# Vision tower with routed experts: expert tiles of 256 rows instead of 128, groups of 30, 25 and 10 token tiles

## The chip, the cores and the metric

One core of one Trainium2 chip. The metric is the device time of one execution in microseconds (us), the median of three runs.

## The reference, cut to what matters

Input x has 32 images of 256 channels, 64 x 64 pixels. A tokenizer turns patches of 4 x 4 pixels into 256 tokens an image by a small attention inside each patch; a class token is put ahead. Then come a tanh recurrence over the images and, last, a mixture of 8 experts on 32 x 257 = 8224 tokens of 256 channels:

```python
logits = tokens.astype(jnp.float32) @ router_w.astype(jnp.float32).T
probs = jax.nn.softmax(logits, axis=-1)
rw, re = jax.lax.top_k(probs, TOP_K)          # TOP_K = 2
rw = rw / jnp.maximum(rw.sum(-1, keepdims=True), 1e-12)
combine = jnp.zeros((N, E), tokens.dtype).at[jnp.arange(N)[:, None], re].set(rw)
out = tokens
for e in range(E):                            # E = 8
    h = jax.nn.gelu(tokens @ w1[e] + b1[e], approximate=False)
    y = h @ w2[e] + b2[e]
    out = out + combine[:, e:e + 1] * y
```

The tokens of the experts are layer-normed; their output is added to the stream before the norm.

## The kernel before

**Two blocks.** The first, the tokens stage, runs 64 units of 128 tokens through a software pipeline of 69 slots (`over_slots`), plus a 65th token tile with the 32 class tokens. In slot k tile k-4 gets its norm, its router logits, and is stored to DRAM twice: `base_dram` (the stream, with the token added) and `rows_dram` (the normed rows).

**Routing by groups.** The 65 token tiles are cut into groups of SIZES = 26, 24, 15. When a group's logits are there, `route_piece` (line 347) works on DVE in eight pieces, one a slot (`pieces_now`, in slots FIRST+SIZE+4 and on): softmax, the best two experts, ranks within an expert (`route_ranks`, PE), and from them for each token two slots in a table sorted by expert, each expert's part rounded up to whole tiles of 128 rows. `experts_of` writes the expert of each tile to `etab`. A group of n token tiles has at most (256 n + 8 x 127) // 128 expert tiles: 59, 55, 37, together 151. `xs_dram` is that table, one for each group; it is cleared with zeros by SP in pieces of three tiles, one a slot, and then `scatter` (line 301) writes each token's row to its two slots with two indirect DMAs from POOL. Group 0 is scattered in the tokens stage (two token tiles a slot in slots 38 to 50), the others at the start of the second block. `weights_high` and `weights_low` split the 64-fold weights into two float16 halves in slots 65 to 68.

**The expert stage** (the second block) has a step k for each expert tile, written out for each engine in its own order:

- SP (one queue, in order): `load_x(k + AHEAD)` into one of XT buffers; `store_y(k - 1)`; `load_base(t)` for the finals whose step is k + 4; `store_out(t)` for those whose step is k - 3.
- PE: `turn_x(k + 4)`, transposes of x in float32; `first(k + 2)`, twelve matmuls of 128 columns with high and low halves of x and w1 (lines 1404 to 1406); `second(k)`, six matmuls of 256 columns (1418 to 1420); then it reads the expert of tile k + 3 to a register (`expert`).
- ACT: `turned(k + 4)`, the float16 copy of the transposed x (1351); `gelus(k + 2)`, two gelus of 128 columns to g32 (1362).
- DVE: `y_in(k - 1)` (1459), bias added; `halves(k + 1)`, a cast of g32 to gh (1443) and the rest to gl (1445); `low(k + 4)`, the low half of x (1449); then `final(t)` (1463) for the finals of step k.
- POOL: scatters of groups 1 and 2, each with its row load, then for all token tiles `gather(t)` (1323): two indirect DMAs that fetch the two y rows of each token.

`final(t)` multiplies the two gathered rows by their gates: mid = y1 * gate + base (1467), fin = y2 * gate + mid (1472). y1, y2, hb and fin have RF = 5 buffers each. So the gather of t waits for f_done of t-5, `load_base(t)` waits for f_mid of t-5 (1287), and fin of t waits until the store of t-5 has landed (1471). The gathers of a group wait until all its y tiles are stored. `final_step` (1250) spreads the finals of groups 0 and 1 evenly over the tiles of the group behind; the 15 of the last group (`LATE`) follow after the last step.

XT, AHEAD, YS are 10, 7 and 6. PSUM: two banks for transposes (TT), three for the first layer (L1), two for y (Y).

Of the kernel before, what the change touches and what calls it, by code (L numbers as in the profile page):

```python
# [38 lines left out]
ROW = 2 * C  # L39
# [71 lines left out]
def vit_tower(nc, xc_in, xp_in, cls_tok, ln_q_w, ln_q_b, wqT, ln_kv_w, ln_kv_w_col, ln_kv_b, wk, wvT, projT, proj_b,  # L111
# [3 lines left out]
    xs_dram = [nc.dram_tensor(f"xs{g}_dram", [TILES[g] * P, C], F32, kind="Internal").ap() for g in GROUPS]  # L115
    ys_dram = [nc.dram_tensor(f"ys{g}_dram", [TILES[g] * P, C], F32, kind="Internal").ap() for g in GROUPS]
    ctx = ExitStack()
    with ctx:
# [28 lines left out]
        cnt = {n: sb(n, [P, E]) for n in "ke kr kf off off128 upto".split()}  # L147
# [153 lines left out]
        def scatter(pool, t, xrow=xrow, xrow_in=xrow_in, sent=sent, first=0):  # L301
# [5 lines left out]
            pool.wait_ge(clear[g], 16 * ((TILES[g] + 2) // 3))  # L307
# [39 lines left out]
        def route_piece(dve, g, part):  # L347
# [47 lines left out]
            if part == 5:  # L395
                dve.wait_ge(s["rk_done"], g + 1)
                step(dve.tensor_scalar(cnt["ke"][:, :], ranks_s[:, n * E:(n + 1) * E], 1.0 / P, (P - 1.0) / P - 0.49609375,
# [5 lines left out]
                step(dve.tensor_scalar(cnt["off128"][:, :], cnt["off"][:, :], float(P), None, ALU.mult))  # L403
            if part == 6:
                step(dve.tensor_tensor(S["rk"], ranks_s[:, 0:n * E].rearrange("p (t e) -> p t e", e=E),
                                       cnt["off128"][:, :].unsqueeze(1).to_broadcast([P, n, E]), ALU.add))
# [28 lines left out]
        def _(sp):  # L435
# [29 lines left out]
            pieces = [(g, q, min(q + 3, TILES[g])) for g in GROUPS for q in range(0, TILES[g], 3)]  # L465
# [746 lines left out]
        LAST = SIZES[-1]  # L1212
# [4 lines left out]
        xt = [sb(f"xt{i}", [P, C]) for i in range(XT)]  # L1217
        xT = [sb(f"xT{i}", [P, ROW], F16) for i in range(3)]
        g32 = [sb(f"g32_{i}", [P, C]) for i in range(2)]
        gh = [sb(f"gh{i}", [P, C], F16) for i in range(2)]  # L1220
        gl = [sb(f"gl{i}", [P, C], F16) for i in range(2)]
        y_s = [sb(f"y_s{i}", [P, C]) for i in range(YS)]
# [7 lines left out]
        names = "tt_ps xl_done xT_done l1_ps g_done gh_done gl_done y_ps y_done f_mid f_done".split()  # L1230
# [26 lines left out]
        LATE = range(T_ALL - LAST, T_ALL)  # L1257
# [9 lines left out]
        def _(sp):  # L1267
            def load_x(sp, k):
# [9 lines left out]
                sp.dma_start(xt[k % XT][:, :], xs_dram[g][j * P:(j + 1) * P, :]).then_inc(x_in[k % XT], 16)  # L1278

            def store_y(sp, k):  # L1280
                g, j = tile_of(k)
                sp.wait_ge(s["y_done"], k + 1)
                sp.dma_start(ys_dram[g][j * P:(j + 1) * P, :], y_s[k % YS][:, :]).then_inc(y_out[k % YS], 16)
# [62 lines left out]
        def _(act):  # L1346
            def turned(act, k):
# [3 lines left out]
                act.activation(xT[k % 3][:, 0:C], TT[k % 2][:, 0:C], ACT.Copy).then_inc(s["xT_done"], 1)  # L1351

            def gelus(act, k):
# [5 lines left out]
                if k >= 2:  # L1359
                    act.wait_ge(s["gl_done"], k - 1)  # L1360
                for m in range(CC):
                    act.activation(g32[k % 2][:, m * P:(m + 1) * P], L1[k % 3][:, m * P:(m + 1) * P], ACT.Gelu,  # L1362
                                   bias=b1_s[:, bass.ds(e, 1), m:m + 1].rearrange("p e n -> p (e n)"),
                                   scale=1.0 / WSC).then_inc(s["g_done"], 1)
# [12 lines left out]
        def _(pe):  # L1377
            mm = pe.matmul

            def turn_x(pe, k):  # L1380
# [3 lines left out]
                for q in range(CC):  # L1384
                    last = pe.transpose(TT[k % 2][:, q * P:(q + 1) * P], xt[k % XT][:, q * P:(q + 1) * P], ident[:, :])  # L1385
# [8 lines left out]
            def first(pe, k, e):  # L1394
                pe.wait_ge(s["xl_done"], k + 1)
                if k >= 3:
                    pe.wait_ge(s["g_done"], 2 * (k - 2))
                for m in range(CC):
                    o = L1[k % 3][:, m * P:(m + 1) * P]
                    for c in range(CC):  # L1400
                        wh = w1h[:, bass.ds(e, 1), c, m * P:(m + 1) * P].rearrange("p e n -> p (e n)")
                        wl = w1l[:, bass.ds(e, 1), c, m * P:(m + 1) * P].rearrange("p e n -> p (e n)")
                        xh, xl = xT[k % 3][:, c * P:(c + 1) * P], xT[k % 3][:, C + c * P:C + (c + 1) * P]
# [5 lines left out]
            def second(pe, k, e):  # L1409
# [3 lines left out]
                o = Y[k % 2][:, 0:C]  # L1413
                for m in range(CC):
                    h, l = gh[k % 2][:, m * P:(m + 1) * P], gl[k % 2][:, m * P:(m + 1) * P]
                    wh = w2h[:, bass.ds(e, 1), m, :].rearrange("p e n -> p (e n)")
                    wl = w2l[:, bass.ds(e, 1), m, :].rearrange("p e n -> p (e n)")
                    mm(o, h, wh, start=(m == 0), stop=False)  # L1418
                    mm(o, h, wl, start=False, stop=False)  # L1419
                    last = mm(o, l, wh, start=False, stop=(m == CC - 1))  # L1420
# [17 lines left out]
        def _(dve):  # L1438
            def halves(dve, k):
                dve.wait_ge(s["g_done"], 2 * k + 2)  # L1440
# [96 lines left out]
```

## Time and profile before

| | us |
|---|---|
| median of 3 runs (1655.04 to 1662.23) | 1656.12 |
| the profiled execution | 1680.15 |
| its span, first to last instruction | 1678.3 |
| PE busy in the span | 1414.3 (84%) |
| DVE busy | 1099.1 (65%) |
| ACT busy | 806.3 (48%) |
| POOL busy | 708.2 (42%) |
| mean granted TensorE clock | 0.955 |

A row of a group of instructions gives the line, engine, operation, output<-inputs, shapes and count, then busy time, the mean of one in ns, and the idle time ahead of them with what ended it. In order of time a row begins with its start and duration. PE's matmuls are pipelined: the distance between starts tells their pace, not their duration. A clock of 1.00 is 2.4 GHz, 0.50 is 1.2 GHz.

### The profile page before, as it was taken

The numbers are of one execution on the slowest core, as the hardware profiler recorded it, in microseconds if no ns is written. First come the engines' busy times: TensorE is split into PE (matmuls) and PEld (weight loads), VectorE is DVE, ScalarE is ACT, GpSimd is POOL, SyncE is SP. The second block draws the span as 40 slices with busy tenths as digits, with TensorE's granted clock in tenths as the row PEclk, the third lists the DMA queues.
The fourth block names the chain that finished last, engine by engine and source line by source line (L and its number), as shares of the span: only waits on it lengthen the run. The fifth ranks groups of instructions, "written<-read, shape, count | busy, mean of one in ns | idle before, by whom it ended". The sixth has DMA issues, their size and how long they took to land. (4 is left out here: it accounts for less than half of the span.)

```text
span 1678.3 us, 65455 instructions
## 1 busy us (share of the span) xinstructions
PE 1414.3 (84%) x25781; PEld 1083.8 (65%) x25781; DVE 1099.1 (65%) x3070; ACT 806.3 (48%) x2022; POOL 708.2 (42%) x858
## 2 busy tenths in 40 slices
PE   3799999999998989989898989989648888888870
PEld 2577777777777766777676667677536566555550
DVE  3567666766665767866676667777447556776773
ACT  1365565655554655555555556556443333333330
POOL 1233343333333433356655534334147734332536
PEclk9899999999998999999999999999869999999995
DMA  8977787877776876889999786673257646675866
GB/s 285 345 263 279 249 298 259 301 258 272 283 274 241 306 254 237 296 275 316 317 312 324 268 290 257 218 252 133 76 164 229 220 152 182 201 211 172 251 207 178
DMA packets 202089, 415.69 MB, mean 248 GB/s; under 512 B 25952, under 2 KB 126624, under 8 KB 201664
## 3 DMA queue, kind: packets, MB, share of 16 engines
q1 hardware_dynamic: 187504, 372.69, 64.7%
q0 software_dynamic: 14288, 38.82, 7.8%
q8 instruction: 214, 3.51, 0.8%
q14 instruction: 83, 0.68, 0.1%
HBM read 329.52 MB, written 81.89 MB: 245 GB/s over the span
## 5 line engine op out<-in xcount | busy, mean ns | idle before, releaser
L1039 DVE BATCH_NORM_STATS2 st<-xp 128x6 f32<-128x512 f32 x512 | 339.1, 694 | 0.5
L537 POOL TENSOR_TENSOR rs_px<-px_ve,half_neg 128x16 f32<-128x16 f32 x64 | 186.3, 2911 | 296.8 <-DVE px_ve L1044 296.8
L649 ACT ACTIVATE zT<-bank 128x512 f32<-128x512 f32 x256 | 146.2, 598 | 193.0 <-PE bank L872 192.9
L1332 POOL DMA_INDIRECT y<-ys_dram,slot x130 | 125.3, 964 | 188.4 <-DMA ys_dram<-y_s 84.4
L872 PE MATMUL bank<-ident,z_s 128*128 128x128 f32 x1024 | 163.4, 295 | 28.3 <-issue 27.5
L642 ACT ACTIVATE z_s<-bank 128x512 f32<-128x512 f32 x256 | 138.7, 597 | 61.4 <-PE bank L862 61.4
L623 ACT ACTIVATE u<-bank 128x512 f32<-128x512 f32 x256 | 132.2, 603 | 53.6 <-PE bank L812 53.6
L872 PEld LDWEIGHTS bank<-ident,z_s 128*128 128x128 f32 x1024 | 120.8, 149 | 46.9 <-issue 40.2
L832 PE MATMUL bank<-xc,u 128*32 128x64 f32 x8192 | 133.9, 220 | 18.2 <-issue 17.5
L832 PEld LDWEIGHTS bank<-xc,u 128*32 128x32 f32 x8192 | 128.0, 110 | 32.8 <-issue 21.0
L310 POOL DMA_INDIRECT xs_dram<-xrow,slot x130 | 128.4, 988 | 40.3 <-issue 37.5
L1362 ACT ACTIVATE g<-bank,b_s 128x128 f32<-128x128 f32 x302 | 94.6, 363 | 103.9 <-PE bank L1406 99.7
L862 PE MATMUL bank<-xp,pd 64*32 64x256 f32 x4096 | 140.1, 383 | 3.2 <-ACT u L623 3.2
L1404 PE MATMUL bank<-xT,xp 128*128 128x128 f16 x604 | 136.9, 227 | 1.3 <-issue 0.5
L1406 PE MATMUL bank<-xT,xp 128*128 128x128 f16 x604 | 137.1, 227 | 0.0
L1459 DVE SCALAR_TENSOR_TENSOR y_s<-bank,b_rep 128x256 f32<-128x256 f32 x151 | 64.1, 424 | 105.6 <-PE bank L1420 93.5
L1405 PE MATMUL bank<-xT,xp 128*128 128x128 f16 x604 | 133.0, 220 | 0.0
L784 PE MATMUL bank<-xp,spread 128*32 128x256 f32 x2048 | 127.7, 391 | 1.3 <-DVE cvec L1031 1.3
L522 POOL TENSOR_TENSOR q_rs<-q_ve,half_neg 128x1 f32<-128x1 f32 x64 | 35.5, 555 | 216.5 <-DVE q_ve L1056 216.2
L1351 ACT ACTIVATE xT<-bank 128x256 f16<-128x256 f32 x151 | 57.9, 383 | 140.0 <-PE bank L1385 140.0
L1385 PE MATMUL bank<-ident,xt 128*128 128x128 f32 x302 | 62.7, 290 | 69.6 <-issue 55.7
L1108 DVE TENSOR_TENSOR h_s<-bank,rc 128x256 f32<-128x256 f32 x64 | 27.2, 425 | 131.2 <-PE bank L891 131.2
(179 smaller groups left out, 3134.6 us busy)
## 6 DMA issues: line engine op xcount, KB each, us to landing
xp<-xpix SPq DMA_DIRECT2D x256, 512.0 KB
xc<-xg SPq DMA_DIRECT2D x256, 512.0 KB
xt<-xs_dram SPq DMA_DIRECT2D x151, 128.0 KB, 3.3
ys_dram<-y_s SPq DMA_DIRECT2D x151, 128.0 KB, 2.6
xs_dram<-zero SPq DMA_DIRECT2D x49, 384.0 KB, 8.2
base_dram<-h SPq DMA_DIRECT2D x65, 128.0 KB, 7.9
rows_dram<-tok SPq DMA_DIRECT2D x65, 128.0 KB, 7.6
hb<-base_dram SPq DMA_DIRECT2D x65, 128.0 KB, 3.0
```

The costliest lines, as they stand in the source:

```text
L310: pool.indirect_dma_start(xs_dram[g], bass.IndirectOffsetOnAxis(ap=slot_u[k][0:n, t:t + 1], axis=0), xrow[i][0:n, :], None).then_inc(sent[ ...
L537: pool.tensor_tensor(rs_px[:, :], px_ve[:, :], half_neg[:, :], ALU.pow).then_inc(s["px_done"], 1)
L623: act.activation(uv[:, k, :, :, :], BIG[k][:, :].rearrange("p (m a t) -> p m a t", m=CC, t=TS), ACT.Copy).then_inc(s["u_done"], 1)
L642: act.activation(z_s[:, r, 2 * half:2 * half + 2, :].rearrange("p a c -> p (a c)"), BIG[2 * r + half][:, :], ACT.Copy).then_inc(s["z_done" ...
L649: act.activation(zT[:, c, :, :].rearrange("p h (a r t) -> p r h a t", r=2, t=TS)[:, r, :, :, :], BIG[f][:, :].rearrange("p (a h t) -> p h ...
L832: last = mm(SB[32 * k:32 * k + 32, (2 * n + r) * SUB:(2 * n + r + 1) * SUB], u_s[u.two][:, c, g, :, :].rearrange("p h t -> p (h t)"), xc[u ...
L862: last = mm(BIG[2 * r + half][32 * k:32 * k + 32, n * C:(n + 1) * C], pd[64 * r:64 * r + 64, g, :, :].rearrange("p h t -> p (h t)"), xp[v. ...
L872: last = pe.transpose(BIG[f][:, n * P:(n + 1) * P], z_s[:, r, n, c * P:(c + 1) * P], ident[:, :])
L1039: dve.bn_stats(st[:, j, :], xp[u.x][:, 2 * j:2 * j + 2, :].rearrange("p i c -> p c i")).then_inc(s["st_done"], 1)
L1404: mm(o, wh, xh, start=(c == 0), stop=False)
L1405: mm(o, wh, xl, start=False, stop=False)
L1406: last = mm(o, wl, xh, start=False, stop=(c == CC - 1))
```

## The change

An expert tile has WIDE = 256 rows, two to a partition (row 2p and 2p+1 of the table in partition p), so x and y move in transfers of 256 KB, with 2 KB to a partition. The first layer's matmuls move 256 columns for each weight load, the second layer runs twice over halves of the tile. The upper half gh comes from a second gelu on ACT with a float16 output instead of DVE's cast. SIZES become 30, 25, 10, TILES 37, 32, 17 (86 together). XT, AHEAD, YS become 8, 5, 5; RF stays 5. The finals follow a new rule: one each 0.75 step, the first three steps after the last tile of their group, as many as end before the last step.

```diff
-SIZES = [26, 24, 15]
+SIZES = [30, 25, 10]
...
-TILES = [(2 * P * n + E * (P - 1)) // P for n in SIZES]
+WIDE = 2 * P
+TILES = [(2 * P * n + E * (WIDE - 1)) // WIDE for n in SIZES]
...
-            pool.wait_ge(clear[g], 16 * ((TILES[g] + 2) // 3))
+            pool.wait_ge(clear[g], 16 * ((2 * TILES[g] + 2) // 3))
...
-            pieces = [(g, q, min(q + 3, TILES[g])) for g in GROUPS for q in range(0, TILES[g], 3)]
+            pieces = [(g, q, min(q + 3, 2 * TILES[g])) for g in GROUPS for q in range(0, 2 * TILES[g], 3)]
...
-        XT, AHEAD, RF, RX2, YS = 10, 7, 5, 4, 6
+        XT, AHEAD, RF, RX2, YS = 8, 5, 5, 4, 5
...
-        final_step = {FIRST[g - 1] + i: BEFORE[g] + 5 + (TILES[g] - 5) * i // SIZES[g - 1]
-                      for g in GROUPS if g > 0 for i in range(SIZES[g - 1])}
+        ready, final_step = [0.0], {}
+        for t in range(T_ALL):
+            ready.append(max(ready[-1] + 0.75, BEFORE[group_of(t)] + TILES[group_of(t)] + 3.0))
+            if ready[-1] < N:
+                final_step[t] = int(ready[-1]) + 1
...
-        LATE = range(T_ALL - LAST, T_ALL)
+        LATE = range(len(final_step), T_ALL)
...
+                src = xs_dram[g][j * WIDE:(j + 1) * WIDE, :].rearrange("(p i) c -> p i c", i=2)
+                sp.dma_start(xt[k % XT][:, :, :], src).then_inc(x_in[k % XT], 16)
...
-                act.activation(xT[k % 3][:, 0:C], TT[k % 2][:, 0:C], ACT.Copy).then_inc(s["xT_done"], 1)
+                act.activation(xT[k % 3][:, 0, :, :], TT[k % 2][:, :].rearrange("p (c n) -> p c n", c=CC),
+                               ACT.Copy).then_inc(s["xT_done"], 1)
...
+                if k >= 3:
+                    act.wait_ge(s["y_ps"], k - 2)
                 for m in range(CC):
+                    for dst in (g32[k % 2], gh[k % 3]):
+                        act.activation(dst[:, m, :], L1[k % 3][:, m * WIDE:(m + 1) * WIDE], ACT.Gelu,
...
                 for q in range(CC):
+                    for i in range(2):
+                        last = pe.transpose(TT[k % 2][:, (2 * q + i) * P:(2 * q + i + 1) * P],
+                                            xt[k % XT][:, i, q * P:(q + 1) * P], ident[:, :])
...
+                        xh, xl = xT[k % 3][:, 0, c, :], xT[k % 3][:, 1, c, :]
                         mm(o, wh, xh, start=(c == 0), stop=False)
                         mm(o, wh, xl, start=False, stop=False)
                         last = mm(o, wl, xh, start=False, stop=(c == CC - 1))
...
+                for i in range(2):
+                    o = Y[k % 2][:, i * C:(i + 1) * C]
+                    for m in range(CC):
+                        h, l = gh[k % 3][:, m, i * P:(i + 1) * P], gl[k % 2][:, m, i * P:(i + 1) * P]
...
-                dve.tensor_copy(gh[k % 2][:, :], g32[k % 2][:, :]).then_inc(s["gh_done"], 1)
-                dve.wait_ge(s["gh_done"], k + 1)
-                dve.tensor_tensor(gl[k % 2][:, :], g32[k % 2][:, :], gh[k % 2][:, :], ALU.subtract).then_inc(s["gl_done"], 1)
+                dve.tensor_tensor(gl[k % 2][:, :, :], g32[k % 2][:, :, :], gh[k % 3][:, :, :],
+                                  ALU.subtract).then_inc(s["gl_done"], 1)
...
+                dve.scalar_tensor_tensor(y_s[k % YS][:, :, :], Y[k % 2][:, :].rearrange("p (i c) -> p i c", i=2), 1.0 / WSC,
+                                         b2_rep[:, bass.ds(e, 1), :].to_broadcast([P, 2, C]),
+                                         ALU.mult, ALU.add).then_inc(s["y_done"], 1)
```

The routing's constants follow the tile of 256 rows (1/256 in place of 1/128).

## Rows read from the trace of the kernel before

**Rows 1.** In order of time: first and last of the expert stage (start, us)

```profile
1239.53 0.69 PE L1385 MATMUL bank<-ident,xt 128*128 128x128 f32 x2 [5.08 <-DMA xt<-xs_dram]
...
1632.85 0.42 DVE L1459 SCALAR_TENSOR_TENSOR y_s<-bank,b_rep 128x256 f32<-128x256 f32 x1 [0.43 <-issue]
```

**Rows 2.** Busy time by window; columns as in its heading

```profile
core 0: us, PE busy (x) PEld busy (x) DVE busy (x) ACT busy (x) POOL busy (x), PEclk, DMA share, GB/s
...
1420.00:1520.00 100.00, 83.45 (x764) 59.35 (x763) 71.32 (x192) 38.41 (x114) 35.09 (x37) 1.00 0.70 204
1545.00:1625.00 80.00, 67.71 (x619) 47.97 (x618) 62.12 (x166) 31.35 (x93) 44.29 (x46) 1.00 0.83 247
```

**Rows 3.** PE in order of time, one tile

```profile
1376.08 0.41 PE L1385 MATMUL bank<-ident,xt 128*128 128x128 f32 x2 [0.29 <-issue]
...
1377.46 0.27 PE L1418 MATMUL bank<-xp,gh 128*128 x1
...
1378.00 0.27 PE L1420 MATMUL bank<-xp,gl 128*128 x1
1378.60 0.41 PE L1385 MATMUL bank<-ident,xt 128*128 128x128 f32 x2 [0.33 <-issue]
```

**Rows 4.** Groups of ACT and DVE by form, whole span

```profile
L649 ACT ACTIVATE zT<-bank 128x512 f32<-128x512 f32 x256 | 146.2, 598 | 193.0 <-PE bank L872 192.9
...
L1362 ACT ACTIVATE g<-bank,b_s 128x128 f32<-128x128 f32 x302 | 94.6, 363 | 103.9 <-PE bank L1406 99.7 <-DVE gl L1445 4.1
L1351 ACT ACTIVATE xT<-bank 128x256 f16<-128x256 f32 x151 | 57.9, 383 | 140.0 <-PE bank L1385 140.0
...
L1067 DVE TENSOR_TENSOR sm<-bank,fold 128x512 f32<-128x512 f32 x64 | 43.6, 682 | 11.8 <-PE bank L832 11.8
```

**Rows 5.** DVE and SP in order of time, late expert stage and tail

```profile
1601.63 0.48 DVE L1472 SCALAR_TENSOR_TENSOR fin<-y,gate,mid 128x256 f32<-128x256 f32 x1
1602.55 0.42 DVE L1459 SCALAR_TENSOR_TENSOR y_s<-bank,b_rep 128x256 f32<-128x256 f32 x1 [0.44 <-issue]
...
1634.77 1.89 SPq L1288 DMA_DIRECT2D hb<-base_dram  x4
```

**Rows 6.** DMA issues (median us to landing): 1420-1520, 1545-1625, tail, span

```profile
xt<-xs_dram SPq DMA_DIRECT2D x38, 128.0 KB, 3.5
...
tower_out<-fin SPq DMA_DIRECT2D x20, 128.0 KB, 2.9
...
tower_out<-fin SPq DMA_DIRECT2D x19, 128.0 KB, 3.4
...
tower_out<-fin SPq DMA_DIRECT2D x14, 128.0 KB, 2.2
...
xc<-w SPq DMA_DIRECT2D x16, 256.0 KB, 4.2
```

**Rows 7.** A gap of PE in the tokens stage, and the window behind it

```profile
1113.80 1.01 PE L872 MATMUL bank<-ident,z_s 128*128 128x128 f32 x4 [3.08 <-issue]
...
1113.00:1117.00 4.00, 3.20 (x21) 2.49 (x21) 0.79 (x2) 1.45 (x3) 0.00 (x0) 0.57 1.02 408
```

**Rows 8.** POOL in order of time: first and last of the 30 tail gathers

```profile
1635.67 0.94 POOL L1332 DMA_INDIRECT y<-ys_dram,slot  x1 [16.18 <-DMA ys_dram<-y_s]
...
1673.13 0.87 POOL L1332 DMA_INDIRECT y<-ys_dram,slot  x1 [0.30 <-issue]
```

**Rows 9.** DVE in order of time, drain of the tokens stage

```profile
1200.17 3.05 DVE L1163 SCALAR_TENSOR_TENSOR xp<-xc,xp 128x512 f16<-128x512 f32 x4 [0.39 <-ACT xp L696]
```

**Rows 10.** DVE in order of time: pd of two quiet slots, two with scatters

```profile
552.34 0.69 DVE L1099 TENSOR_TENSOR pd<-bank,rs_own 128x512 f32<-128x512 f32 x1 [0.32 <-PE bank L848]
...
568.96 0.69 DVE L1099 TENSOR_TENSOR pd<-bank,rs_own 128x512 f32<-128x512 f32 x1 [0.19 <-PE bank L848]
...
772.43 0.69 DVE L1099 TENSOR_TENSOR pd<-bank,rs_own 128x512 f32<-128x512 f32 x1 [0.30 <-PE bank L848]
...
790.41 0.69 DVE L1099 TENSOR_TENSOR pd<-bank,rs_own 128x512 f32<-128x512 f32 x1 [0.33 <-PE bank L848]
```

More of the change, by code:

```diff
@@ L114, in vit_tower @@
     rows_dram = nc.dram_tensor("rows_dram", [T_ALL, P, C], F32, kind="Internal").ap()
-    xs_dram = [nc.dram_tensor(f"xs{g}_dram", [TILES[g] * P, C], F32, kind="Internal").ap() for g in GROUPS]
-    ys_dram = [nc.dram_tensor(f"ys{g}_dram", [TILES[g] * P, C], F32, kind="Internal").ap() for g in GROUPS]
+    xs_dram = [nc.dram_tensor(f"xs{g}_dram", [TILES[g] * WIDE, C], F32, kind="Internal").ap() for g in GROUPS]
+    ys_dram = [nc.dram_tensor(f"ys{g}_dram", [TILES[g] * WIDE, C], F32, kind="Internal").ap() for g in GROUPS]
     ctx = ExitStack()
@@ L146, in vit_tower @@
         tiny = {n: sb(n, [P, NMAX]) for n in "lmx lsum lrec m1 i1 m2 i2 msum mcl mrec s1 s2".split()}
-        cnt = {n: sb(n, [P, E]) for n in "ke kr kf off off128 upto".split()}
+        cnt = {n: sb(n, [P, E]) for n in "ke kr kf off offw upto".split()}
         offm = sb("offm", [P, E, E])
@@ L402, in route_piece @@
                 step(dve.tensor_reduce(cnt["off"][:, :], offm[:, :, :], X, ALU.add))
[L403 removed]
+                step(dve.tensor_scalar(cnt["offw"][:, :], cnt["off"][:, :], float(WIDE), None, ALU.mult))
             if part == 6:
                 step(dve.tensor_tensor(S["rk"], ranks_s[:, 0:n * E].rearrange("p (t e) -> p t e", e=E),
[L406 removed]
+                                       cnt["offw"][:, :].unsqueeze(1).to_broadcast([P, n, E]), ALU.add))
                 for k in range(2):
@@ L1211, in vit_tower @@
         N = TILES_ALL
-        LAST = SIZES[-1]
         BEFORE = [sum(TILES[:g]) for g in GROUPS]
-        XT, AHEAD, RF, RX2, YS = 10, 7, 5, 4, 6
+        XT, AHEAD, RF, RX2, YS = 8, 5, 5, 4, 5
         xrow2 = [sb(f"xrow2_{i}", [P, C]) for i in range(RX2)]
         b2_rep = sb("b2_rep", [P, E, C])
[L1217 to L1222, printed above, removed]
+        xt = [sb(f"xt{i}", [P, 2, C]) for i in range(XT)]
+        xT = [sb(f"xT{i}", [P, 2, CC, WIDE], F16) for i in range(3)]
+        g32 = [sb(f"g32_{i}", [P, CC, WIDE]) for i in range(2)]
+        gh = [sb(f"gh{i}", [P, CC, WIDE], F16) for i in range(3)]
+        gl = [sb(f"gl{i}", [P, CC, WIDE], F16) for i in range(2)]
+        y_s = [sb(f"y_s{i}", [P, 2, C]) for i in range(YS)]
         y1 = [sb(f"y1_{i}", [P, C]) for i in range(RF)]
@@ L1282, in store_y @@
                 sp.wait_ge(s["y_done"], k + 1)
-                sp.dma_start(ys_dram[g][j * P:(j + 1) * P, :], y_s[k % YS][:, :]).then_inc(y_out[k % YS], 16)
+                dst = ys_dram[g][j * WIDE:(j + 1) * WIDE, :].rearrange("(p i) c -> p i c", i=2)
+                sp.dma_start(dst, y_s[k % YS][:, :, :]).then_inc(y_out[k % YS], 16)
             def load_base(sp, t):
@@ L1412, in second @@
                     pe.wait_ge(s["y_done"], k - 1)
[L1413 to L1420, printed above, removed]
+                for i in range(2):
+                    o = Y[k % 2][:, i * C:(i + 1) * C]
+                    for m in range(CC):
+                        h, l = gh[k % 3][:, m, i * P:(i + 1) * P], gl[k % 2][:, m, i * P:(i + 1) * P]
+                        wh = w2h[:, bass.ds(e, 1), m, :].rearrange("p e n -> p (e n)")
+                        wl = w2l[:, bass.ds(e, 1), m, :].rearrange("p e n -> p (e n)")
+                        mm(o, h, wh, start=(m == 0), stop=False)
+                        mm(o, h, wl, start=False, stop=False)
+                        last = mm(o, l, wh, start=False, stop=(m == CC - 1))
                 last.then_inc(s["y_ps"], 1)
```

24 lines of the change are left out of this document (9 added, 15 removed).

## The prediction

> **What bounds the kernel now.** I read the stages first. The last block, the expert stage, runs from the first transposes that have their data to the end of the last y_s at 1633.3 [rows 1]: 393.8 us for 151 tiles, 2.61 us each, and 45.1 us of tail follow to the end of the span at 1678.3. In the stretches by window [rows 2] PE is busy 83% at full clock while DVE has 71% and the DMA engines 0.70 (third quarter), later 78% and 0.83. Then one tile in order of time [rows 3]: from one pair of transposes to the next 2.52 us. The transposes take 0.24, the first layer with its hand-over 1.14 (12 matmuls of 128 columns), the six second-layer matmuls of 256 columns 0.108 each = 0.65, and from the end of the last one (1378.11) to the next transposes 0.49 go by, PE's register load and waits. So PE's own stream sets the tile; the other 0.09 to 2.61 is small stalls. Not in the rows of before, but in the code: SP runs one queue in which the load of x for a later tile stands behind waits for the final additions.
>
> **The change, part by part.**
>
> *PE step.* Tiles go from 151 to 37+32+17 = 86 of double size. Four transposes 0.53 (two: 0.24 to 0.27), first layer 12 x 256 columns and second 12 x 256, at the second layer's 0.108: 2.59; hand-over 0.11, overhead 0.49, stalls 0.08 as before: 3.80. 86 x 3.80 = 327, and 2 to fill. Taken alone that saves 65 us. Bounds for the pitch of the 256-column first layer: 0.095 (its pitch at 128 columns, 1.14/12) and 0.27, the duration of one 256-column matmul if none overlapped; the second layer's 0.108 is the same shape, so I take it. The Trainium skill ("TensorE: Matmul & The Clock Gate", Back-to-back issue gap) gives 81 ns at 128 columns and 131 at 512; read between, 98 at 256. The case's row says 108 for 256, so the measurement decides; by the page the steps would be 21 us shorter in all.
>
> *ACT, DVE.* ACT per step: one copy of 512 columns at 0.60 (as zT), and four gelus of 256 columns. A copy grew by 0.215 from 256 to 512 columns, so 128 more add 0.11 to the gelu's 0.36: 4 x 0.47 = 1.9. Together 2.5 of 3.8, hidden by PE; two tiles of before took 2.2, so without cover it would cost 0.3 a step. DVE: three operations of 512 elements at 0.68 (as sm), the cast gone: 2.0. A final is mid and fin, 0.5 each [rows 4, 5]. At 4 finals in 3 steps that makes 3.4 per step: hidden, but barely. The second gelu writes gh and waits for y of three tiles earlier, which PE has long finished: nothing; if not, PE's lead over ACT would shrink by part of a step.
>
> *The finals' schedule.* Here the gain goes. Finals now come every 0.75 step (before: about every 2), yet RF is still 5, so unit t-5's final is 3 or 4 steps before t's. final_step becomes 41, 41, 42, 43, 44, 44, 45, 46, 47, 47, ... and from 73 in the same pattern: 30 + 19 units, 16 late.
> (a) load_base(t) stands in SP step final_step-4 and waits for mid of t-5. For every fourth unit that mid is in DVE step k+1, while SP is in step k. Behind it is load_x(k+6), which PE needs at step k+2, and AHEAD is now 5. Mid comes 2.7 into step k+1; SP 0.4 and a landing of 3.9 make 7.0, against 3.8: PE stands 3.2 us.
> (b) store_out(t-5) stands at final_step(t-5)+3, the same step as final(t) or one before, behind load_base. The fin of t waits for that store's landing, and half of the units meet it.
> Once both hold, three steps (four finals) close into a ring: mid frees SP, one hb issue 0.47 and the out landing 2.9: 3.4; fin and the next mid 1.0; again SP and out 3.4; fin 0.5, register gap 0.4, three tile operations 1.9 (they overlap a little), mid 0.5: 3.3; two SP issues 0.9 and x 3.9: 4.8; transposes and drain 0.83, ACT's copy 0.65, low and mid 1.2: 2.7. Sum 18.6, 6.2 per step against 3.8 [rows 3 to 6]. The landing of 256 KB isn't shown for x: 128 KB took 3.5, a 256 KB weight load 4.2; I take 3.9, ends 3.5 and 4.5.
> The ring needs t-5 to exist: in each group the first two rounds (steps 42, 45) pay only 3.2, 4 x 3.2 = 13; then steps 47 to 60 and 79 to 85 pay 2.4 each, 21 x 2.4 = 50. Queued behind: store_y and every x load on SP; gathers on POOL wait for fin, 2.6 a unit against 4.7 available, hidden.
>
> *Clock.* In the tokens stage PE stood 3.08 us and then ran with a granted clock of 0.57 for the next 4 us, mostly the lower level of 1.2 GHz [rows 7]. PE would now stand 3 to 5 us eleven times. In the ring PE has 7 us of slack in three steps, only its transposes are on the path. Per stall 0.5 (transposes at half speed) to 3.3 (a whole step's extra): I take 0.8, 9 us; ends 0 and 36.
>
> *Expert stage*: 327 + 2 + 13 + 50 + 9 = 401, +7 against 393.8.
>
> *Tail.* Before, POOL waits for the last y store and then issues 30 gathers at 1.29 [rows 8], last issue to end 5.2. After, the last y_s is followed by four stores, hb(49), final(49): 6.2 until gather(54) may start, then 11 units x 2.58, less one gather 1.3, plus 5.2: 38.5. -7.
>
> *Before the expert stage.* Routing pieces of group 1 move from slots 54 to 61 to 59 to 66. Pieces 6 and 7 fall into the drain, where DVE had 0.39 us of idle before the weight halves [rows 9]: five to seven small operations, 2.4 and 1.7, less the idle: +3 (0 to 5). x loads of 256 KB around the 1 MB b2 load: +1. Group 0 scatters in 15 slots instead of 13; a slot with scatters is 18.0 us (pd to pd), a quiet one 16.6 [rows 10]: +3. Seven more clears of 384 KB lie beside PE: 0 (to 5). Routing group 2 in the expert stage gets shorter, n 10 for 15, hidden either way. Group 1's 25 scatters have until step 32, when SP loads its first tile, 4.9 us for a unit of two indirect DMAs: hidden; the cover gone would show as a stop before tile 37.
>
> *Sum*: +7 -7 +3 +1 +3 = +7 on the profiled execution's 1680.15 (span 1678.3 in it): 1687. The median of the runs, 1656.12, is 24 lower; the same difference gives **1663**.
>
> **The rivals.**
> *Long landings, cold array (slower).* For it: with the DMA engines fuller the out landing was 3.4 [rows 6], and eleven stalls of over 3 us. Landings 0.4 longer in three places: ring +1.2 to 1.4, seven rings, +10. Clock 25 instead of 9. Expert stage 427, sum +33: 1689. It decides where the stalls leave the clock low through the following step, so that PE, not SP, closes the ring. Against it: PE's slack in the ring. The Trainium skill (same page, HAM oscillation) describes a loop whose DMA waits make every iteration start throttled; by that rule this case is the likely one. The one row here agrees that such a gap lowers the clock.
> *Short landings (faster).* In the tail, with the same kind of traffic, out landed in 2.2 [rows 6]. Ring 18.6 - 1.4 - 0.5 = 16.7, 5.6 per step: 21 x 1.8 = 37, early rounds 11, clock 0: 377. Sum -17: 1639.
> *The ring does not bind (faster).* If SP were never late (waits met earlier than I count), 329: -65, sum -65: 1591. DMA would then hold it up a bit: 1.2 MB per 3.8 us, over the 247 GB/s that 0.83 busy gave in the last finals of before; so rather 1605. Against it: the waits are written out, and the step numbers give no slack.
>
> **How the numbers follow.** Forecast (ring, 1645 to 1677) 0.45; slow rival 0.25; short landings 0.20; no ring 0.10. The range leaves out the no-ring case and the far end of the slow one: 1628 to 1697. What a measurement can tell from no change is 0.5%, 8.3 us (1647.8 to 1664.4). Faster: no ring, short landings and a little of the forecast, 0.33; same 0.25, slower 0.42, since 1663 is near the upper bound and the slow rival is all beyond it.
>
> **What would show it.** Right: matmuls of the first layer 0.108 apart; steps of 3.8 in the first 40 tiles; between steps 42 and 60 and from 74 on, about 6.2; SP waiting for DVE mid in load_base by some 90 us in total; DVE fin waiting for DMA tower_out by over 40; PE's transposes waiting for DMA xt about eleven times; a granted clock under 1 in both stretches; a tail of 38. Wrong: steps under 4.3 in the finals, or SP's waits for mid near zero (no ring); PE busy all through at 0.5 clock (slow rival); first-layer matmuls over 0.14 apart; or a tokens stage more than 10 us longer.

## Result: 1.35% faster, and where the time came from

The median of twelve runs went from 1659.0 us (1653.1 to 1671.4) to **1639.6 us** (1630.1 to 1652.2), a ratio of 0.9865 with a 95% interval of 0.9839 to 0.9891. The forecast was 1663, slightly slower: the range (1628 to 1697) holds the result, but the direction is wrong.

| | before | after |
|---|---|---|
| profiled execution, us | 1680.15 | 1630.14 |
| its span | 1678.3 | 1628.3 |
| PE busy | 1414.3 (84%) | 1362.7 (84%) |
| DVE busy | 1099.1 (65%) | 1043.5 (64%) |
| ACT busy | 806.3 (48%) | 839.9 (52%) |
| mean granted clock | 0.955 | 0.945 |
| tokens stage, to the first transposes with data | 1239.5 | 1224.1 |
| expert stage | 393.8 | 362.9 |
| tail | 45.1 | 41.3 |

The two profiled executions are not alike: that of before was 21 us above its own median, that of after was the fastest of its twelve. So 50 us lie between the two spans and only 19 between the medians. The tokens stage shows that chance: in kernels of this study that share its code to the letter the start of the expert stage went from 1223 to 1238. What can be read from one profile each is the expert stage and the tail. The unchanged new kernel, profiled twice more, gave expert stages of 371.9 and 369.8.

**PE in the first part of the expert stage**, in order of time, the rows that answer to [rows 3]:

```profile
1300.94 0.60 PE L1394 MATMUL bank<-ident,xt 128*128 128x128 f32 x4
1301.38 0.27 PE L1414 MATMUL bank<-xT,xp 128*128 128x256 f16 x1
1301.49 0.27 PE L1415 MATMUL bank<-xT,xp 128*128 128x256 f16 x1
...
1302.58 0.27 PE L1416 MATMUL bank<-xT,xp 128*128 128x256 f16 x1
1302.69 0.27 PE L1429 MATMUL bank<-xp,gh 128*128 x1
...
1303.89 0.27 PE L1431 MATMUL bank<-xp,gl 128*128 x1
1304.00 0.60 PE L1394 MATMUL bank<-ident,xt 128*128 128x128 f32 x4
```

Transposes 0.44, then 24 matmuls 0.109 apart with nothing between first and second layer, and the next transposes one pitch behind the last matmul: a step is 3.06 us, not 3.80. The 0.49 between tiles of [rows 3] is gone. The same stretch of before shows where its first layer lost time. The three matmuls of a triple (L1404 to L1406) start 0.056 apart, then the next triple comes late:

```profile
1376.32 0.22 PE L1404 MATMUL bank<-xT,xp 128*128 128x128 f16 x1
1376.38 0.22 PE L1405 MATMUL bank<-xT,xp 128*128 128x128 f16 x1
1376.43 0.22 PE L1406 MATMUL bank<-xT,xp 128*128 128x128 f16 x1
1376.62 0.23 PE L1404 MATMUL bank<-xT,xp 128*128 128x128 f16 x1
```

Ahead of the transposes of before PE stood idle with nothing in the profile to wait for ("issue"), 142 times between 1240 and 1640; in after no such row is left:

```profile
PE bank L1385 <- issue: 55.7, 142, 0.8
```

**The finals**: busy time by window (columns as in its heading), for [rows 2]. The first window lies in the finals of group 0, the second in the ten steps without finals, the third in the finals of group 1:

```profile
core 0: us, PE busy (x) PEld busy (x) DVE busy (x) ACT busy (x) POOL busy (x), PEclk, DMA share, GB/s
1384.00:1475.00 91.00, 58.87 (x413) 46.76 (x412) 46.73 (x87) 32.13 (x75) 39.21 (x40) 0.86 0.68 201
1478.00:1520.00 42.00, 40.75 (x369) 36.32 (x367) 29.16 (x49) 28.24 (x66) 9.35 (x10) 1.00 0.66 214
1545.00:1585.00 40.00, 22.40 (x167) 17.56 (x165) 20.74 (x40) 11.20 (x27) 19.65 (x22) 0.86 0.67 201
```

With finals no engine is busy over two thirds of the time, and the DMA engines are at 0.68: everything waits for something. For what, the waits say (engine, line, releaser: us in total, times, longest), first those of SP's queue, then the others of the expert stage:

```profile
SPq L1287 <- DVE y_s L1470: 166.5, 74, 15.6
SPq L1292 <- DVE mid L1478: 82.0, 36, 4.6
```

```profile
DVE fin L1483 <- DMA tower_out<-fin: 60.3, 23, 6.5
PE bank L1394 <- DMA xt<-xs_dram: 54.5, 28, 4.3
```

**One turn of the ring**, SP, DVE and the transposes in order of time:

```profile
1425.17 0.47 DVE L1478 SCALAR_TENSOR_TENSOR mid<-y,gate,hb 128x256 f32<-128x256 f32 x1
1425.67 5.01 SPq L1292 DMA_DIRECT2D hb<-base_dram  x2
1426.10 0.48 DVE L1483 SCALAR_TENSOR_TENSOR fin<-y,gate,mid 128x256 f32<-128x256 f32 x1 [0.46 <-DMA tower_out<-fin]
...
1429.86 0.47 DVE L1478 SCALAR_TENSOR_TENSOR mid<-y,gate,hb 128x256 f32<-128x256 f32 x1
...
1430.72 1.47 SPq L1297 DMA_DIRECT2D tower_out<-fin  x1
...
1432.24 0.43 SPq L1281 DMA_DIRECT2D xt<-xs_dram  x1
...
1433.67 0.48 DVE L1483 SCALAR_TENSOR_TENSOR fin<-y,gate,mid 128x256 f32<-128x256 f32 x1 [3.34 <-DMA tower_out<-fin]
1434.07 0.48 DVE L1478 SCALAR_TENSOR_TENSOR mid<-y,gate,hb 128x256 f32<-128x256 f32 x1
...
1435.47 1.12 PE L1394 MATMUL bank<-ident,xt 128*128 128x128 f32 x4 [4.27 <-DMA xt<-xs_dram]
```

SP issued one hb load at 1425.67 and then stood in the second until the mid of 1429.86; only then went the store of fin (1430.72) and the load of x (1432.24) that stood behind it. DVE's next fin waited 3.34 for that store, PE's transposes 4.27 for that load. These are the two waits (a) and (b) of the prediction. Starts of y_s every third step (1384.37, 1401.89, 1420.22, 1438.31, 1457.98, 1474.58) are 18.0 apart in the mean; forecast 18.6.

**The tail**, DVE, SP and POOL in order of time:

```profile
1586.31 0.69 DVE L1470 SCALAR_TENSOR_TENSOR y_s<-bank,b_rep 128x512 f32<-128x512 f32 x1 [0.37 <-issue]
...
1587.40 2.45 SPq L1297 DMA_DIRECT2D tower_out<-fin  x5
...
1589.89 2.05 SPq L1292 DMA_DIRECT2D hb<-base_dram  x4
...
1594.76 0.48 DVE L1478 SCALAR_TENSOR_TENSOR mid<-y,gate,hb 128x256 f32<-128x256 f32 x1 [6.85 <-DMA hb<-base_dram]
...
1596.28 0.95 POOL L1336 DMA_INDIRECT y<-ys_dram,slot  x1 [5.37 <-DVE fin L1483]
```

### The profile page after: what moved, and what is told of

Read it like the earlier page. It is cut to its first block and busy times, and to the rows that moved or that the text cites. A ratio compares the mean times of both kernels' runs of the same rounds, so it can differ in the third digit from the quotient of the medians.

```text
span 1628.3 us, 61722 instructions
## 1 busy us (share of the span) xinstructions
PE 1362.7 (84%) x25169; PEld 1088.0 (67%) x25169; DVE 1043.5 (64%) x2724; ACT 839.9 (52%) x1999; POOL 709.9 (44%) x854
## 3 DMA queue, kind: packets, MB, share of 16 engines
q8 instruction: 204, 3.34, 0.8%
## 5 line engine op out<-in xcount | busy, mean ns | idle before, releaser
L872 PE MATMUL bank<-ident,z_s 128*128 128x128 f32 x1024 | 158.5, 288 | 23.8 <-issue 23.1
L872 PEld LDWEIGHTS bank<-ident,z_s 128*128 128x128 f32 x1024 | 117.3, 145 | 45.1 <-issue 38.2
L1370 ACT ACTIVATE g<-bank,b_s 128x256 f32<-128x256 f32 x172 | 82.0, 477 | 77.3 <-PE bank L1416 75.6
L1394 PE MATMUL bank<-ident,xt 128*128 128x128 f32 x344 | 58.6, 297 | 65.9 <-DMA xt<-xs_dram 65.5
L1051 DVE BATCH_NORM_STATS2 qst<-rT 128x6 f32<-128x256 f32 x64 | 27.3, 426 | 127.2 <-ACT rT L604 127.2
L1429 PE MATMUL bank<-xp,gh 128*128 x344 | 97.6, 284 | 8.1 <-DVE gl L1454 8.1
L1470 DVE SCALAR_TENSOR_TENSOR y_s<-bank,b_rep 128x512 f32<-128x512 f32 x86 | 59.4, 691 | 67.7 <-PE bank L1431 50.1
L1415 PE MATMUL bank<-xT,xp 128*128 128x256 f16 x344 | 100.1, 291 | 0.0
L1416 PE MATMUL bank<-xT,xp 128*128 128x256 f16 x344 | 100.0, 291 | 0.0
```

Of the source, the lines that this page charges most:

```text
L872: last = pe.transpose(BIG[f][:, n * P:(n + 1) * P], z_s[:, r, n, c * P:(c + 1) * P], ident[:, :])
L1415: mm(o, wh, xl, start=False, stop=False)
```

## The experiments

All times are medians, and ratios are to the kernel before on the same chip; the expert stage is read from each run's profile. Runs marked single were executed once. They stood on two other chips, where the kernel before took 1736 and 1738, nearly 5% above its median, so no total of theirs is compared and only structure is read from them.

**The changed kernel again**, on two chips, as the base for the others.

> The changed kernel once more, as the base for the others on the same chip. Every theory: ratio to before 0.987 (0.98 to 0.995); a step of 3.06 us before the first final, about 18 us for three steps in the finals (ring), expert stage 355 to 370 us. The part ahead of the expert stage is what differs between profiled executions: the two so far were 15 us apart there; if that was the kernel, it shows again (over 10 us shorter than before), if it was chance it does not.

> The changed kernel again, as the base for the three beside it. Every theory: ratio to before 0.987 to 0.995, expert stage 360 to 375 us, steps 41 to 60 at 5.9 to 6.1.

Measured: 1648.3, ratio 0.9927 (0.9903 to 0.9950), expert stage 371.9; and 1642.3, ratio 0.9851 (0.9813 to 0.9889), expert stage 369.8: at and just over the upper end of what was expected. Waits as above: SP for mid 87.0 and 85.0, fin for its store 63.4 and 64.0, PE for x 63.7 and 63.0.

**Undoing the ring.** Eight buffers in place of five for y1, y2, hb and fin:

```diff
-        XT, AHEAD, RF, RX2, YS = 8, 5, 5, 4, 5
+        XT, AHEAD, RF, RX2, YS = 8, 5, 8, 4, 5
```

> RF 8 in place of 5: unit t-8's final is six steps back, so that neither SP's load_base nor DVE's fin has anything to wait for. Ring theory: SP's waits for mid (82 us) and fin's waits for tower_out (60 us) fall under 10 each, the finals' steps go from 6.0 to what DVE needs, 2.0 + 0.35 + 1.33 = 3.7 us, and the expert stage shrinks by 60 to 75 us: about 295 us, device time 1565 to 1585. Rival (DMA engines are full in the finals, the waits only show it): a step has 1.2 MB to move, at the 298 GB/s seen that is 4.0 us, and landings grow; the steps stay above 4.5 and the gain is under 45 us. Rival (clock): the granted clock stays under 0.9 in the finals and the gain is under 45 us.

Measured: **1577.4**, ratio 0.9490 (0.9456 to 0.9524), expert stage 304.2: 71 us under the same kernel with five. The waits of SP's queue:

```profile
SPq L1287 <- DVE y_s L1470: 178.8, 84, 16.1
SPq L1281 <- PE bank L1394: 3.9, 4, 1.9
SPq L1292 <- DVE mid L1478: 2.7, 4, 1.4
```

and busy time in a stretch without finals and one with them:

```profile
1310.00:1350.00 40.00, 38.96 (x355) 35.00 (x353) 24.66 (x40) 27.57 (x64) 29.54 (x33) 1.00 0.86 278
1368.00:1440.00 72.00, 60.78 (x520) 51.73 (x519) 55.12 (x101) 40.29 (x93) 55.52 (x55) 0.98 0.95 311
```

The wait for mid fell from 87.0 to 2.7, fin no longer waits for a store, and from y_s 40 to y_s 60 it takes 79.2 us where it took 121.0. The stretch before (y_s 0 to 40) is the same, 129.4 and 128.7. What is left in the finals is 3.96 a step with the DMA engines at 0.95 and 311 GB/s; over the whole stage PE waits 29.6 us for x. That looks like the transfer limit of the rival without a ring, but it is not yet a floor: the last version below takes 3.68 a step.

**The pace of the finals** instead of the buffers, one per step:

```diff
-            ready.append(max(ready[-1] + 0.75, BEFORE[group_of(t)] + TILES[group_of(t)] + 3.0))
+            ready.append(max(ready[-1] + 1.0, BEFORE[group_of(t)] + TILES[group_of(t)] + 3.0))
```

> Finals every step in place of every 0.75, RF still 5: unit t-5's final is five steps back, load_base's wait is met a step earlier. 43 finals in the steps, 22 late instead of 16. Ring theory: no waits for mid or tower_out over 10 us, steps of 3.4 at most in the finals, expert stage 275 to 290 us (-75 to -85), tail 6 units longer, +10 to +16: device time 1565 to 1585. Rival (full DMA or POOL sets the finals): steps stay above 4.

Measured: 1590.8, ratio 0.9566 (0.9520 to 0.9612). SP waits 1.6 for mid, fin for no store; the expert stage is 297.5, shorter than with eight buffers, but more finals are left over and the tail is 52.7. So a second way out of the ring, with the buffers untouched, brings 57 of the 71 us: the ring, not the buffers' size as such, held the stage. The stage was expected at 275 to 290 and the total at 1565 to 1585; both came out 6 to 8 us above the upper end, with 3.61 us a step from y_s 40 to y_s 60 where 3.4 at most was expected.

**The two waits apart.** Eight buffers for fin alone (fin8 single, fin8_b repeated), and for hb alone:

```diff
+        RO = 8
...
-        fin = [sb(f"fin{i}", [P, C]) for i in range(RF)]
+        fin = [sb(f"fin{i}", [P, C]) for i in range(RO)]
...
-                if t >= RF:
-                    dve.wait_ge(out_done[q], 16 * (t // RF))
+                if t >= RO:
+                    dve.wait_ge(out_done[t % RO], 16 * (t // RO))
```

```diff
+        RH = 8
...
-        hb = [sb(f"hb{i}", [P, C]) for i in range(RF)]
+        hb = [sb(f"hb{i}", [P, C]) for i in range(RH)]
...
-                if t >= RF:
-                    sp.wait_ge(s["f_mid"], t - RF + 1)
+                if t >= RH:
+                    sp.wait_ge(s["f_mid"], t - RH + 1)
```

> Eight fin buffers and their semaphores, all other rings of five: takes away fin's wait for the store of t-5 alone. Ring theory: waits for tower_out go from 60 to under 10; SP still waits for mid of t-5, so PE still waits for x every third step: cycle 0.9 + 3.9 + 2.7 + two steps of 3.06 = 13.6 instead of 18.0, expert stage -30 to -40 us. Rival (the stores' waits hide behind the x waits): under -15 us.

> Eight fin buffers alone, beside a base on the same chip. The first look had fin's waits at zero, SP's for mid at 57 us and steps 41 to 60 at 5.36. Ring theory, mended by that look: the x part stays, -10 to -15 us against the changed kernel, steps 41 to 60 at 5.2 to 5.5. Rival (the two waits carry half each): -30 us or more.

> Eight hb buffers alone: SP's load_base waits for mid of t-8, so SP is free, fin still waits for the store of t-5, which SP now issues on time. Theory (SP's blocked queue is what delays both the x load and the stores): nearly the whole gain of the kernel with RF 8, -55 to -70 us, waits for tower_out under 15. Rival (the fin ring has a wait of its own): tower_out still over 30 us, gain under 45.

| | us | ratio | expert stage | SP for mid | fin for store | PE for x |
|---|---|---|---|---|---|---|
| five of each (again3) | 1642.3 | 0.9851 | 369.8 | 85.0 | 64.0 | 63.0 |
| fin 8 | 1622.2 | 0.9682 (0.9604 to 0.9759) | 343.2 | 74.7 | 0 | 51.5 |
| hb 8 | 1601.9 | 0.9597 (0.9530 to 0.9665) | 321.2 | 4.8 | 29.1 | 31.0 |

With fin 8 the store's wait is gone and 20 us with it; SP still stands in front of mid. That lies between the two theories (10 to 15, and 30 or more), and the first expectation, 30 to 40 less in the expert stage, was too high as well. With hb 8 SP is free and 40 us go; but the fin buffers keep a wait of their own (19 times, 29.1 us), where the theory had under 15 us of it and a gain of 55 to 70. The rival, that fin has a wait of its own and the gain stays under 45, is nearer. So both waits carry a part, the one for mid the larger. The run with eight of each, on another chip, gave 71; it has eight y1 and y2 as well, and no run here tells whether the 11 us over 20 + 40 are theirs. The single run of fin 8 showed the same structure (57.1, none, 53.5).

**x one step further ahead**, AHEAD 6 in place of 5:

```diff
-        XT, AHEAD, RF, RX2, YS = 8, 5, 5, 4, 5
+        XT, AHEAD, RF, RX2, YS = 8, 6, 5, 4, 5
```

> AHEAD 6 in place of 5: x is asked for one step earlier, so PE's waits for xt (54 us) fall under 10. Ring theory: the ring closes without x by DVE's own steps: 3.4 + 1.0 + 3.4 + 3.3 and two DVE steps of 3.3, 17.7 instead of 18.0 us; the early rounds gain 4 x 3: expert stage -10 to -20 us in all. Rival (the x load behind SP's wait is what costs): -40 us or more.

Single. In the expert stage PE still waits 32.7 us for x (under 10 were expected), now 15 times, fin 56.6 for its store, SP for mid 52.6; steps 41 to 60 are 5.74 in the mean where the new kernel has 5.9 to 6.1. One step of lead moves the stalls and doesn't open the ring. Whether it brings the 10 to 20 us that were expected isn't shown, as there is no base on that chip.

**The sizes of the groups** back at 26, 24 and 15, all else new:

```diff
-SIZES = [30, 25, 10]
+SIZES = [26, 24, 15]
```

> Groups of 26, 24, 15 with tiles of 256 rows: 33, 31, 22 tiles, 86 as well; 15 late units, all of group 2 and none of group 1. My terms say: tokens stage 3 us shorter (13 slots with scatters), drain 3 us shorter, five more finals of group 1 in the ring (+8 to +12), tail 45 instead of 41 (+4): together 1 to 10 us slower than the changed kernel. Rival: the grouping does nothing, within 3 us. Rival: long groups cost in the tokens stage, and this one is over 8 us faster.

Measured: 1646.9, ratio 0.9900 (0.9865 to 0.9936), against 1648.3 on the same chip: no difference, as the rival "the grouping does nothing" had it. The tail is 44.9 instead of 40.9, the expert stage 370.4 instead of 371.9. What the smaller last group gains at the end is not seen in the total.

**Why a PE step is 3.06, not 3.80.** Call the stream of PE's own instructions, as against the matmuls that the array works off, its instruction side. Three things could have made the array wait in before: the register load (with the expert's number), the instructions that work out the weights' addresses from that register, or the handshakes between engines. First, the first layer of the new kernel cut back to 128 columns, 24 matmuls instead of 12:

```diff
+                    for i in range(2):
+                        oi, h = o[:, i * P:(i + 1) * P], slice(i * P, (i + 1) * P)
...
-                        mm(o, wh, xh, start=(c == 0), stop=False)
+                            mm(oi, wh, xh, start=(c == 0), stop=False)
```

> The first layer of the changed kernel with 24 matmuls of 128 columns instead of 12 of 256, all else equal. Read before the first final, where a step is 3.06 us and PE never idle. The 0.49 us that PE lost between tiles in the kernel before, theory A (PE's instruction stream is the limit there: 20 matmuls with their loads take 2.52 us to issue, 0.126 each, and 256 columns hide it): 40 matmuls need 4.5 to 5.0 us a step. Theory B (a wait of its own, for the register with the expert, which the longer step covers): 24 at 0.09 instead of 12 at 0.109, a step of 3.9 or less.

Single. Steps between transposes, from 1290 to 1380 and so ahead of the finals: median 3.46, fastest tenth 3.09. Theory A (each matmul costs 0.126 us of the instruction side) needed 4.5 to 5.0 and fell. In the fast steps the matmuls of 128 columns stand 0.056 apart, here all 24 in a row:

```profile
1332.31 0.22 PE L1416 MATMUL bank<-xT,xp 128*128 128x128 f16 x1
1332.37 0.22 PE L1417 MATMUL bank<-xT,xp 128*128 128x128 f16 x1
...
1333.59 0.22 PE L1418 MATMUL bank<-xT,xp 128*128 128x128 f16 x1
1333.65 0.27 PE L1431 MATMUL bank<-xp,gh 128*128 x1
```

So the array takes 128 columns in half the time of 256, and the 0.095 of [rows 3] was not its pace. Now the kernel before, with nothing changed but where the expert comes from. In three of these every tile uses one and the same expert, so the choice of the expert by tile is left out (b_again leaves nothing out):

```diff
-                return pe.value_load(etab[g][0:1, j:j + 1], min_val=0, max_val=E - 1)
+                return 0
```

> The kernel before with PE using expert 0 for every tile, no register load on PE (leaves out the choice of the expert's weights). Theory A (instruction stream): the tile falls only by the few register instructions, 2.61 to 2.4 or more, and PE's idle time at the transposes stays over 0.2 us a tile. Theory B (the register load is a wait of its own after the second layer): the gap of 0.49 us goes, a tile is 2.1 us or less and the expert stage 70 us shorter.

> The kernel before once more, as the base of this call. Every theory: median distance of two tiles' transposes 2.52 us, expert stage 385 to 400 us.

```diff
-                return pe.value_load(etab[g][0:1, j:j + 1], min_val=0, max_val=E - 1)
+                pe.value_load(etab[g][0:1, j:j + 1], min_val=0, max_val=E - 1)
+                return 0
```

> The kernel before with the expert loaded to PE's register for each tile but weights at fixed addresses (expert 0 for all: leaves out the choice of weights). Theory L (the load is the wait): gap of about 0.5 between tiles stays, first layer 0.056 apart, a tile about 2.0 to 2.1 at the median. Theory S (the address instructions): 1.54 to 1.65 at the median where nothing else waits.

```diff
-                return pe.value_load(etab[g][0:1, j:j + 1], min_val=0, max_val=E - 1)
+                if not once:
+                    once.append(pe.value_load(etab[g][0:1, j:j + 1], min_val=0, max_val=E - 1))
+                return once[0]
```

> The kernel before with one expert register for all tiles, loaded at the first (leaves out the choice of weights): matmuls still take their addresses from registers, but no load and few address instructions a tile. Theory L and theory S both: 1.54 to 1.7 at the median. If operands addressed by register are slow in themselves: 2.0 or more.

All are single; b_const ran on another chip than the three others. Steps between transposes over the whole expert stage, in us:

| kernel before with | median | fastest tenth | expert stage |
|---|---|---|---|
| nothing changed (b_again) | 2.62 | 2.46 | 451.0 |
| the register load kept, its value not used (b_load) | 2.31 | 1.55 | 384.5 |
| one register for all tiles (b_reg1) | 2.41 | 1.54 | 378.7 |
| no register (b_const) | 2.19 | 1.54 | 364.7 |

For b_again a median of 2.52 and a stage of 385 to 400 were expected. On that chip other stalls, whose cause wasn't followed up, lengthen the stage, so the fast steps are what to compare.

The list of PE's instructions says what differs. A tile of before has a register load, then one address instruction ahead of each L1404 and each L1406 matmul (eight) and one ahead of each L1418 and L1419 (four). With one register the twelve stand there once for the whole stage and the matmuls go on using them; with the constant they are gone; with the load kept and its value unused, the load alone is left. The fastest tenth of all three is 1.55, that of before 2.46. So the load by itself doesn't hold the array (that theory fell), and matmuls with addresses in registers aren't slow in themselves: without the twelve **address instructions** a tile is 0.9 us shorter. The handshakes between engines are the same in all four kernels, so they aren't it either.

That is not what they cost. The trace of before has a record for each of PE's register instructions, which the views leave out. In the tile of [rows 3] the eight address instructions of the first layer start 0.124 apart (one pair 0.19), the four of the second layer 0.11 to 0.15; with two semaphore waits between them they take the time from 1376.20 to 1377.85, 1.65 us. There the register load begins, and 0.72 us later, at 1378.57, the next transposes' first weights are loaded: the gap of 0.49 lies in this time. With the 0.15 from there to the next address instruction that is the whole 2.52. So **PE's instruction side had no slack in before, and address instructions and load together set the tile**. Without the addresses an estimate of it from these distances is 2.52 - 8 x 0.124 - 4 x 0.113 = 1.1, less than the array's own 1.55, which is what is left. No run here takes out the load alone.

PE in order of time, with constant addresses:

```profile
1380.42 0.27 PE L1420 MATMUL bank<-xp,gl 128*128 128x256 f16 x1
1380.53 0.38 PE L1385 MATMUL bank<-ident,xt 128*128 128x128 f32 x2
1380.75 0.22 PE L1404 MATMUL bank<-xT,xp 128*128 128x128 f16 x1
1380.81 0.22 PE L1405 MATMUL bank<-xT,xp 128*128 128x128 f16 x1
```

No gap ahead of the transposes, 0.056 between matmuls. The waits of PE between 1290 and 1600, unchanged and with the load kept:

```profile
PE bank L1385 <- issue: 33.6, 88, 1.1
```

```profile
PE bank L1419 <- issue: 30.1, 44, 2.2
PE bank L1385 <- issue: 9.7, 38, 0.5
PE bank L1419 <- DVE gl L1446: 8.7, 13, 1.2
```

Freed of them, the tile of before is held elsewhere (ahead of the second layer, on DVE's gl and on "issue"), which is why the medians stay at 2.2 to 2.4. Last, the same edit in the new kernel (expert 0 for all):

> The changed kernel with expert 0 for all tiles on PE, no register load and fixed addresses (leaves out the choice of weights). Instruction side hidden behind the array in the changed kernel: the step before the finals stays 3.06 (3.00 to 3.10) and the ring stays at 18 us for three steps. If the instruction side still cost there: 2.9 or less.

Single: median step 3.15 ahead of the finals, fastest tenth 3.05, steps 41 to 60 6.11. Nothing changed: the new tile has as many address instructions, twelve, and the same register load, at the same distances in the trace of after (0.124 and 0.113), but 24 matmuls of 0.109 each to hide them under. The run with 24 first-layer matmuls of 128 columns agrees: it too has twelve, and they are hidden although each matmul lasts only 0.056. What counts is the array's work in a tile (3.06 and 3.09, against 1.55 in before) beside its instruction side (2.52 in before).

**A version without the ring and with more lead**, RF 8, AHEAD 6, XT 9:

```diff
-        XT, AHEAD, RF, RX2, YS = 8, 5, 5, 4, 5
+        XT, AHEAD, RF, RX2, YS = 9, 6, 8, 4, 5
```

> RF 8 with AHEAD 6 and XT 9: in the kernel with RF 8 PE still waited 30 us for xt. If those waits were the prefetch distance: -15 to -25 us more, device time 1553 to 1563. Rival (DMA engines 0.95 busy at 311 GB/s in the finals set the pace): within 6 us of the kernel with RF 8.

Measured: **1560.4**, ratio 0.9346 (0.9303 to 0.9390), 82 us under the changed kernel on the same chip and 108 under the kernel before. Expert stage 287.0; busy time without and with finals:

```profile
1290.00:1350.00 60.00, 60.00 (x552) 54.63 (x550) 38.95 (x66) 42.14 (x99) 43.66 (x50) 1.00 0.90 289
1360.00:1430.00 70.00, 64.75 (x566) 56.61 (x565) 57.79 (x106) 43.60 (x101) 54.12 (x53) 0.98 0.97 328
```

PE is busy all the time in the first, the DMA engines are at 0.97 in the second. With the ring open the extra step of lead is worth something: against RF 8 alone PE's wait for x goes from 29.6 to 11.5, the expert stage from 304.2 to 287.0. The total lies in the expected 1553 to 1563. The two ran on different chips, so the part of the extra lead in it is known only roughly: over the changed kernel on the same chip the gain is 82 where RF 8 alone had 71. The DMA engines are now the fullest in the finals, but no run here takes transfers away: that they set the pace there is argued, not shown.

## Why the prediction was wrong

The expert stage by stretches, cut at starts of y_s. "Forecast" is the prediction's own sum laid over them, without its 9 us for the clock:

| stretch | forecast | after | again | eight buffers |
|---|---|---|---|---|
| first transposes to y_s 0 | 6 | 10.4 | 10.2 | 10.2 |
| y_s 0 to 40, no finals | 152 | 126.1 | 128.7 | 129.4 |
| 40 to 60, finals of group 0 | 116 | 118.1 | 121.0 | 79.2 |
| 60 to 72, none | 46 | 37.4 | 38.5 | 37.8 |
| 72 to end, finals of group 1 | 73 | 70.9 | 73.6 | 47.6 |

**The PE step: wrong, and this decided it.** The step of the prediction that failed is "overhead 0.49 ... as before" with its hand-over 0.11 and the sum 3.80: it carried the time between tiles over as a constant of a step. Measured 3.06 = 0.44 + 24 x 0.109. Over the 52 steps without finals that is 34 us in these stretches. The runs show what stood in its place: PE's instruction side, twelve address instructions and a register load. In before it took 2.52 us a tile against the array's 1.55 and set the tile; after has the same twelve and the same load, and the array's 3.06 is longer and hides them. A step is the longer of the two, not the array's work plus an overhead. It was to be read from before: in the tile of [rows 3] the first-layer matmuls of a triple are 0.056 apart and the triples begin 0.24 to 0.30 apart, and the prediction took the mean of both, 0.095, for a pitch. Larger tiles don't save array work: 86 x 3.06 are 263 us where 151 x 1.55 are 234, as the table has 22016 rows in place of 19328. They save instruction side: its register instructions come once a tile.

**The first layer at 256 columns, 0.108**: right (0.109). The Trainium skill ("TensorE: Matmul & The Clock Gate", Back-to-back issue gap) gives 81 ns at 128 columns for a sustained stream and 131 at 512. These runs don't agree at 128, where a fed stream had 56; an estimate read between the two gives 98 for 256 columns, and they took 109. What they agree with is the formula that the same section keeps for an isolated matmul, about N/2.4 + 2.5 ns: 56 and 109.

**ACT and DVE**: right. A gelu of 256 columns took 477 ns (forecast 0.47), DVE's operations on 512 elements 683 to 691 (0.68), both hidden.

**The finals' ring**: right in mechanism, place and size. 18.0 us per three steps for 18.6. The six parts of that sum, read in the turn from the end of the mid at 1430.33 to the end of the one at 1448.70, are 3.3, 0.9, 2.9, 3.1, 5.7 and 2.4 where 3.4, 1.0, 3.4, 3.3, 4.8 and 2.7 were forecast: the x load took longer, all else less. SP waited 82 to 87 for mid (90), fin 60 to 64 for its store (over 40). PE's transposes waited for x 27 to 32 times, not eleven: in the ring nearly every step's load is late, not only each third. The runs with eight buffers (-71), with slower finals (-57), and with eight hb or fin (-40, -20) show that the ring held what its waits say, SP's blocked queue being the larger part. Opened, it gave 68 us of the expert stage (371.9 to 304.2): with five buffers it took that much of a gain of 90 (393.8 to 304.2). The forecast of the stretches with finals, 189, came true (189 and 195 measured) because PE's own step has hardly a part in the ring.

**The clock**: 9 us forecast. The granted clock did fall to 0.86 in both stretches (first transposes of a step at half speed, 1.12 for 0.60, in the rows of the ring above), as the slow rival had it, but the ring's period has no 9 us over in it. No run here takes the clock's part by itself.

**Tail**: -4 instead of -7. The order was as forecast, but mid waited 6.85 for its hb, and gather(54) began 9.3 after the end of the last y_s, not 6.2.

**Ahead of the expert stage**: routing pieces 6 and 7 did fall into the drain (2.4 and 1.5 us of DVE ahead of the weight halves). The +7 can't be read from one profile each, since its start varies by 15 us with no change; the medians less expert stage and tail (1659 - 394 - 45, and 1640 - 368 - 41, with the mean of the three profiles) leave 1220 and 1231, which doesn't speak against it. So the +7 is argued, not shown.

**The rivals.** Long landings fell: steps in the ring were not longer than forecast. "Short landings" gave the right time, 1639, for a wrong reason: out landed in 3.0 within the ring, not 2.2. The case without a ring, at 1605 and not 1591 because DMA would hold it, is what eight buffers showed: 1577, transfers at 0.95, its PE step being too long as well.

**The sum**: the forecast stood at +7 on the expert stage, where the three profiles have -22 to -31; of this -34 from the steps without finals, -9 from the clock, +4 from filling the pipeline. That the stated range holds 1639.6 is due to its width and to a ring that came as forecast, not to the PE step.

## What to carry to other kernels

Split the idle time and the mean pitch of an engine into what comes per instruction, per tile and per byte before they are carried over to another tile size. Matmuls in even triples with gaps between them, here, were an instruction side that fell behind; more array work per tile hid it, and the step is the longer of the two. When tiles get larger and fewer, count again in steps what was counted in steps before (buffer rings, leads, the pace of work woven in), and read the waits along one queue: a load that waits for a buffer holds every load and store behind it. A ring of waits has a period of its own; no engine's time shows in it, and only opening it does.

## What was not expected of the hardware

An instruction that works out an address from a register for a matmul takes 0.11 to 0.12 us of PE's instruction side, and from the start of a register load to the next weights it is 0.72. With 18 matmuls a tile, leaving out the twelve address instructions brings the fast tiles from 2.46 to 1.55; with 24 matmuls of 256 columns leaving out both brings nothing (3.05 with and without). Fed in time, float16 matmuls of 128 columns follow each other in 0.056 us, those of 256 in 0.109. The 16 DMA engines moved 311 to 328 GB/s at 0.95 to 0.97 busy with this mix of 256 KB and 128 KB transfers and gathers, and with eight buffers stores of 128 KB landed in 4.4 us where the ring had 3.0.
